# Layer 0 context attention of a four-layer perceiver on Trainium2: features laid out by halves of the heads, rotation without a matmul, the inverse root by logarithm, exponential and a Newton step

## The chip, the cores and the metric

The program runs on one core of one Trainium2 chip. The metric is the device time of one execution in microseconds. The core has a matrix engine (PE, with weight loads PEld beside it), a vector engine (DVE), an activation engine (ACT), a general engine (POOL) and a queue that issues transfers (SP), each working through its own instructions in order; semaphores make one wait for another.

## The reference, cut to what matters

Twelve stages of four layers run one after another on x (4 batches of 256 tokens with 256 features). The change is in the first stage, attention of x to a context of 4 x 4096 rows with 16 heads of 16 features, where queries and keys are normalised and rotated per head:

```python
def rms_norm(x, w):
    var = jnp.mean(x * x, axis=-1, keepdims=True)
    return x * jax.lax.rsqrt(var + EPS) * w

def apply_rope(t, cos, sin):
    t1, t2 = jnp.split(t, 2, axis=-1)
    return jnp.concatenate([t1 * cos - t2 * sin, t2 * cos + t1 * sin], axis=-1)
```

The query (from x) and the key (from the context) of each head go through `rms_norm` and then `apply_rope`; the rest is softmax attention, with scores scaled by a quarter, and an output projection that is added to x.

The other eleven stages are the same in both kernels. Layers 1 and 2 have context attentions of their own, which share code with this one but take its branches without rotation.

## The kernel before, in words

`context_attention` (called by `l0_xattn` with rope=True) works in two steps.

**The projection stage**, `project_first`, makes all queries (2 chunks of 512 columns) and the keys and values of batch 0 (8 chunks). A chunk holds two units, one for each 128 of the 256 features; a unit is 128 features by 512 tokens, and there are 20. For a unit PE multiplies (L1944) and, for keys, makes two tiles of values (L1953); ACT copies the product with the norm's weight (L1979) and squares it (L1980); PE sums the squares within each head by a block matrix (L1933) and exchanges the halves of the heads by a turn matrix (L1934); ACT takes the root of the mean square (L1993); DVE multiplies by cosine (L2009) and, from PSUM, by sine (L2011), adds (L2015) and inverts the root (L2017); POOL applies it (L2041). Then the float32 result is split in three bfloat16 parts, by ACT (L1971), DVE (L2023) and POOL (L2046, L2048), and SP stores them (L1908 for keys, L1913 for queries). The splitting of a unit stands behind the rotation of the next on every engine.

**The batches.** `attend_context` runs once per batch b = 0 to 3. It goes over 16 heads with 8 slots each (e = 0 to 7). In a slot PE makes a 128 x 1024 piece of scores (`scores`, L2343) and weighs the values with the exponentials of the slot before (`weigh`, L2360); ACT takes the exponentials (L2519). Beside that, PE computes the next head's scores a first time (`guard`, 16 pieces of 512 columns per head, L2314, placed by the table GUARDS, up to three per slot), of which DVE takes maxima (L2431). In slot 7 the maxima become a shift (L2328 on PE, the copy L2443 on DVE), and the output of an earlier head is finished (L2373, L2448, L2451). Before the first head a stretch with all 16 guards of head 0 runs alone. SP loads each head's keys, three transfers that each repeat rows of DRAM over several partitions (`load_keys`, L2229): those of head h + 2 once the scores of head h - 1 are done, and in head 15 those of the following batch's first head.

Batches 0 to 2 also make the next batch's keys and values, one unit per head, through the methods of `NextKeys`. Unit h + 1 is made in head h: projection in slots 0 and 1 (L2114), the head sum in slot 2 (`sum_heads`, L2121), the turn in slot 3 (`turn_pairs`, L2126), values in slots 5 and 6 (L2137), all in one PSUM bank. ACT copies and squares (L2151, L2152) before the exponential of slot 2 and takes the root (L2158) before that of slot 3; DVE multiplies by sine (L2182) in slot 4, inverts the root in four quarters (L2188, slots 5 to 7 and 0) and takes the rest (L2194) in slot 3 of the head after; POOL does the cosine product, sum, norm and the two lower parts (L2205 to L2221); SP stores a unit with one transfer (L2099) and loads context and table for two units at a time (L2090, L2095). The order on each engine is written by hand:

```python
if h + 2 < H:
    if h >= 1:
        sp.wait_ge(qk, EU * h)
    load_keys(sp, keys, kstack, h + 2, slot(h + 2), k_in[(h + 2) % 3])
...
if following and h == H - 1:
    new.first_heads_stored(sp)
    sp.wait_ge(qk, EU * (H - 2))
    load_keys(sp, following[1], kstack, 0, slot(H), following_in)
```

`output_product` (L2548 to L2568) ends each batch. Then the next batch's block begins, with the memset L2427 as DVE's first instruction.

## Time and profile before

| what | before |
|---|---|
| median of 3 runs | 7321.39 us (7313.24 to 7321.71) |
| profiled execution, its own time | 7326.7 us |
| span of the profiled execution | 7324.9 us, 101148 instructions |
| busy: PE / DVE / ACT / POOL | 6076.4 / 4217.8 / 3224.1 / 1042.4 us |
| mean granted clock of PE | 0.907 |
| this stage: projection | about 24 to 212 us of the span |
| this stage: batches 0, 1, 2, 3 start at | 212.1, 554.0, 892.8, 1232.2 us |

The profile comes from one execution. An engine is busy while one of its instructions runs; a mean over the span mixes stages with different limits, so a stretch is read by itself. The granted clock is a share of PE's full speed. In a timeline a row gives start, duration, engine, source line, operation, and in brackets the idle time ahead of it and what ended that. Matmuls of float32 count as two records each.

### The profile page before, as it was taken

Reading aid. Unit: us, or ns where it says so; the run is one execution under the profiler, and the core shown is the slowest. Engines: PE = TensorE matmul, PEld = TensorE weight load, DVE = VectorE, ACT = ScalarE, POOL = GpSimd, SP = SyncE. Lnnn points to the kernel's source line nnn. Section 1 sums busy time; section 2 is a strip of 40 time slices with the busy share of each in tenths; the row PEclk is TensorE's granted clock in tenths of the full one; section 3 lists DMA queues with packets and bytes.
Section 4 is the critical chain, followed back from the end, with each engine's and each line's share of the span. In section 5 each row is a group of like instructions: output and inputs, shape, how many; then the busy total and the mean of one; then the engine's idle time right before and its main releaser. Section 6 shows DMA issues by size and latency. Waiting matters only on the chain. (4 is left out here: it accounts for less than half of the span.)

```text
span 7324.9 us, 101148 instructions
## 1 busy us (share of the span) xinstructions
PE 6076.4 (83%) x35500; PEld 3373.9 (46%) x35500; DVE 4217.8 (58%) x8493; ACT 3224.1 (44%) x7821; POOL 1042.4 (14%) x1122
## 2 busy tenths in 40 slices
PE   6799999978288379999998897878877998987887
PEld 3344444423155245454445554333333565556754
DVE  8777787839311236666673332988987445535631
ACT  3566665510033125454453111988987223532211
POOL 4222221004423420000000002110100000001100
PEclk8899999979699689999998898999988678998998
DMA  3323231130288432222210113322321000022100
GB/s 114 92 74 96 78 91 61 51 107 0 99 259 258 134 115 85 75 79 79 64 53 28 36 35 106 97 85 83 97 62 61 1 1 7 1 84 67 49 19 24
DMA packets 281228, 550.02 MB, mean 75 GB/s; under 512 B 29726, under 2 KB 186789, under 8 KB 261909
## 3 DMA queue, kind: packets, MB, share of 16 engines
q1 hardware_dynamic: 262388, 493.46, 22.6%
q0 software_dynamic: 18336, 50.09, 1.9%
q8 instruction: 286, 4.69, 0.3%
q14 instruction: 218, 1.78, 0.1%
HBM read 414.73 MB, written 128.75 MB: 74 GB/s over the span
## 5 line engine op out<-in xcount | busy, mean ns | idle before, releaser
L2431 DVE TENSOR_REDUCE t<-banks 128x1 f32<-128x512 f32 x2048 | 1373.3, 690 | 369.7 <-PE banks L2314 302.8
L2519 ACT ACTIVATE t<-banks 128x1024 f32<-128x1024 f32 x1024 | 1044.2, 1025 | 768.1 <-PE banks L2343 763.3
L2747 ACT ACTIVATE t<-banks,t 128x256 f32<-128x256 f32 x2048 | 939.9, 529 | 77.7 <-DVE t L2684 55.0
L2314 PE MATMUL banks<-t 96*128 96x512 bf16 x2048 | 796.2, 394 | 109.9 <-PEq L66 59.4
L2684 DVE TENSOR_REDUCE t<-banks 128x4 f32<-128x1024 f32 x512 | 623.7, 1219 | 97.3 <-PE banks L2630 56.7
L2360 PE MATMUL banks<-t 128*17 128x256 f32 x8192 | 641.7, 385 | 20.8 <-ACT t L2519 17.5
L2343 PE MATMUL banks<-t 97*128 97x256 bf16 x4096 | 651.4, 273 | 0.0
L2747 ACT ACTIVATION_READ_ACCUMULATOR t<-banks,t 128x1 f32 x2048 | 512.5, 261 | 0.0
L2343 PEld LDWEIGHTS banks<-t 97*128 97x128 bf16 x4096 | 390.6, 98 | 256.7 <-issue 112.2
L2643 PE MATMUL banks<-t 128*17 128x256 f32 x4096 | 327.1, 405 | 160.8 <-DVE t L2695 109.2
L2314 PEld LDWEIGHTS banks<-t 96*128 96x128 bf16 x2048 | 198.7, 97 | 558.6 <-DVE t L2431 333.5
L2630 PE MATMUL banks<-t 96*128 96x256 bf16 x2048 | 328.1, 286 | 50.8 <-PEq L66 25.4
L2219 POOL CAST t<-t 128x512 bf16<-128x512 f32 x144 | 87.7, 609 | 1874.7 <-DVE t L2194 1874.7
L2114 PE MATMUL banks<-xn_feat,t 128*128 128x512 f32 x576 | 321.4, 642 | 13.7 <-issue 6.7
L2137 PE MATMUL banks<-t,xn_feat 128*128 128x256 f32 x1152 | 317.5, 398 | 1.1 <-DVE t L2182 1.1
L1556 ACT ACTIVATE t<-banks,t 128x256 f32<-128x256 f32 (+1 forms) x384 | 171.9, 453 | 331.6 <-DVE t L1522 331.5
L2630 PEld LDWEIGHTS banks<-t 96*128 96x128 bf16 x2048 | 185.1, 103 | 264.5 <-ACT t L2747 155.1
L1522 DVE TENSOR_REDUCE t<-banks 128x1 f32<-128x256 f32 (+1 forms) x384 | 136.6, 398 | 280.8 <-PE banks L1658 158.1
L1198 DVE TENSOR_TENSOR t<-banks,t 128x192 f32<-128x192 f32 x127 | 45.5, 358 | 435.8 <-ACT t L1179 435.8
L2360 PEld LDWEIGHTS banks<-t 128*17 128x17 f32 x8192 | 136.1, 95 | 314.1 <-issue 254.6
L575 PE MATMUL banks<-t 128*128 128x256 f32 x1024 | 239.5, 391 | 32.1 <-DMA t<-in_ctxT 32.1
L2137 PEld LDWEIGHTS banks<-t,xn_feat 128*128 128x128 f32 x1152 | 205.4, 191 | 102.2 <-issue 58.9
(418 smaller groups left out, 10058.8 us busy)
## 6 DMA issues: line engine op xcount, KB each, us to landing
t<-in_L_ffn_w SPq DMA_DIRECT2D x127, 640.0 KB, 5.3
scratch_k<-t SPq DMA_DIRECT2D x192, 384.0 KB, 15.0
t<-scratch_k SPq DMA_DIRECT2D x192, 384.0 KB
t<-scratch_k SPq DMA_DIRECT2D x192, 256.0 KB
xn_feat<-in_ctxT SPq DMA_DIRECT2D x72, 512.0 KB, 15.7
t<-in_ctxT SPq DMA_DIRECT2D x56, 512.0 KB
t<-scratch_k SPq DMA_DIRECT2D x192, 128.0 KB
t<-in_L_ffn_w SPq DMA_DIRECT2D x18, 1024.0 KB
```

The costliest lines, as they stand in the source:

```text
L575: mm = nc.tensor.matmul(out, ctx[:, ch % 2, k, (2 * i + t) * P:(2 * i + t + 1) * P], wkv[:, k, kind * C:(kind + 1) * C], start=k == 0, sto ...
L2114: mm = self.core.nc.tensor.matmul(self.out, self.w[:, k, f * P:(f + 1) * P], self.ctx[:, c % 2, k, :], start=k == 0, stop=k == CT - 1)
L2137: mm = nc.tensor.matmul(self.v_out[:, t * C:(t + 1) * C], self.ctx[:, c % 2, k, (2 * f + t) * P:(2 * f + t + 1) * P], self.w_v[:, k, :], s ...
L2314: mm = nc.tensor.matmul(ps[:, 4 + g % 2, :], qstack[0:SHIFT, h, t * P:(t + 1) * P], kstack[0:SHIFT, slot(h), kc * KC:(kc + 1) * KC], start ...
L2343: mm = nc.tensor.matmul(out, kstack[:, slot(h), kt * P:(kt + 1) * P], qstack[:, h, :], start=True, stop=True, skip_group_check=bool(near))
L2360: mm = nc.tensor.matmul(ps[PART * j:PART * j + VW, OUT, 0:T], v[:, 4 * e + j, h, :], p[:, i % 3, j * T:(j + 1) * T], start=e == 0, stop=e ...
L2431: nc.vector.tensor_reduce(gm[:, h % 2, g // NK, g % NK:g % NK + 1], ps[:, 4 + g % 2, :], AX.X, ALU.max).then_inc(max_done, 1)
L2519: nc.scalar.activation(p[:, i % 3, :].rearrange("p (b t) -> p b t", b=2), ps[:, 2 * (i % 2):2 * (i % 2) + 2, :], ACT.Exp).then_inc(exp_don ...
L2630: mm = nc.tensor.matmul(ps[:, 2 * (i % 3) + j // 2, (j % 2) * T:(j % 2 + 1) * T], kstack[0:SHIFT, slot(h), kt * P:(kt + 1) * P], qstack[0: ...
L2643: mm = nc.tensor.matmul(ps[PART * j:PART * j + VW, OUT, 0:T], scaled[:, i % SL, j, :], p[:, i % SL, j * T:(j + 1) * T], start=e == 0, stop ...
L2684: nc.vector.tensor_reduce(nm[:, i % 4, :], ps[:, 2 * (i % 3):2 * (i % 3) + 2, :].rearrange("p b (j t) -> p (b j) t", j=2), AX.X, ALU.max, ...
L2747: nc.scalar.activation(p[:, i % SL, j * T:(j + 1) * T], ps[:, 2 * (i % 3) + j // 2, (j % 2) * T:(j % 2 + 1) * T], ACT.Exp, bias=nm[:, i % ...
```

## The change

Queries and keys of layer 0 get their features in another order in the weights: the first halves of all 16 heads are unit 0 of a chunk, the second halves unit 1. The partner of a feature in the rotation is then the same partition of the other unit, so the turn matmul goes, and the sine product reads the other unit's copy in SBUF. The head sum becomes one accumulated pair of matmuls per chunk with a block matrix of eights, and root, mean and inverse are made once per chunk. The inverse root is exp(-0.5 ln(m)) on ACT followed by a Newton step of three DVE instructions, in place of a square root and a reciprocal; ln and exp come from one table set, loaded once per phase. In the batches the rotation moves to POOL altogether (six products and sums per chunk, then two for the norm), units run two heads ahead instead of one, and the units of a chunk are stored together, with three transfers per unit instead of one, in every second head. In the projection stage the rotation stays on DVE. The non-rotating branches of `project_first` and `NextKeys` keep their instructions. The core of the diff, stage by stage (projection on PE, ACT and DVE; the new class RopeKeys; then SP, PE, DVE and ACT of `attend_context`; the layout):

```diff
+                    pe.wait_ge(copied, CT * (c + 1))
+                    for f in range(CT):
+                        mm = nc.tensor.matmul(ps[:, 4 + c % 2, :], pairs, square[:, f, :], start=f == 0, stop=f == CT - 1)
...
+                nc.scalar.preload_act_table_set(EXP_AND_LN)
...
+                    act.wait_ge(summed, c + 1)
...
+                    nc.scalar.activation(mean[:, c % 2, :], ps[:, 4 + c % 2, :], ACT.Identity, bias=eps,
+                                         scale=1.0 / D).then_inc(mean_done, 1)
+                    nc.scalar.activation(root[:, c % 2, :], ps[:, 4 + c % 2, :], ACT.Ln, bias=eps,
+                                         scale=1.0 / D).then_inc(log_done, 1)
+                    nc.scalar.activation(root[:, c % 2, :], root[:, c % 2, :], ACT.Exp, scale=-0.5).then_inc(root_done, 1)
...
+                    for f in range(CT):
+                        nc.vector.tensor_tensor(mix[:, s, f, :], raw[:, s, f, :], tab[:, s, 0, :],
+                                                ALU.mult).then_inc(cos_done, 1)
+                    for f in range(CT):
+                        nc.vector.tensor_tensor(spun[:, f, :], raw[:, s, 1 - f, :], tab[:, s, 1, :],
+                                                ALU.mult).then_inc(sin_done, 1)
+                    for f in range(CT):
+                        nc.vector.tensor_tensor(mix[:, s, f, :], mix[:, s, f, :], spun[:, f, :],
+                                                ALU.subtract if f == 0 else ALU.add).then_inc(mixed, 1)
...
+                    link(nc.vector.tensor_tensor(mean[:, s, :], mean[:, s, :], root[:, s, :], ALU.mult))
+                    link(nc.vector.scalar_tensor_tensor(out=mean[:, s, :], in0=mean[:, s, :], scalar=-0.5,
+                                                        in1=root[:, s, :], op0=ALU.mult, op1=ALU.mult))
+                    nc.vector.scalar_tensor_tensor(out=root[:, s, :], in0=mean[:, s, :], scalar=1.5, in1=root[:, s, :],
+                                                   op0=ALU.add, op1=ALU.mult).then_inc(refined, 1)
...
+def half_rows(dest, part, c, f):
+    return dest[part].rearrange("(h two d) n -> two h d n", two=2, d=D // 2)[f, :, :, c * KC:(c + 1) * KC]
...
+    def store(self, sp, u):
+        sp.wait_ge(self.low_done, u + 1)
+        for part in range(3):
+            sp.dma_start(half_rows(self.dest, part, u // CT, u % CT), self.parts[:, u % 2, part, :]).then_inc(
+                self.stored[u % 2], 16)
...
+    def first_heads_stored(self, sp):
+        self.all_stored(sp)
...
+    def product_used(self, pe, u):
+        pe.wait_ge(self.copied, u + 1)
+        if u % CT == CT - 1:
+            pe.wait_ge(self.mean_done, u // CT + 1)
+            pe.wait_ge(self.log_done, u // CT + 1)
...
+            nc.gpsimd.tensor_tensor(self.mix[:, f, :], self.raw[:, f, :], self.tab[:, s, 0, :], ALU.mult).then_inc(
+                self.cos_done, 1)
+            nc.gpsimd.tensor_tensor(self.spun[:, 1 - f, :], self.raw[:, f, :], self.tab[:, s, 1, :], ALU.mult).then_inc(
+                self.sin_done, 1)
...
-                        if (h + 1) % CT == 0 and (h + 1) // CT + 1 < new.chunks:
-                            new.load_chunk(sp, (h + 1) // CT + 1)
-                        new.store(sp, h)
+                        if h % CT == 1 and (h + 3) // CT < new.chunks:
+                            new.load_chunk(sp, (h + 3) // CT)
+                        if h % CT == 0:
+                            for f in range(CT):
+                                new.store(sp, h + f)
...
+                    if new and rope and g in (2, 4):
+                        if g == 4:
+                            new.product_used(pe, 0)
+                        for k in range(CT):
+                            new.multiply(pe, g // 2 - 1, k)
+                    if new and rope and g == 6:
+                        new.sum_heads(pe, 0)
...
-                    u = h + 1
+                    u = h + lead
-                    if new and rope and u < H and e == 2:
-                        new.sum_heads(pe, u)
-                    if new and rope and u < H and e == 3:
-                        new.turn_pairs(pe, u)
+                    if new and rope and u < H and e == 3 and u % CT == CT - 1:
+                        new.sum_heads(pe, u // CT)
...
-                    if new and rope and e == 3:
-                        new.take_rest(dve, u - 1)
-                    if new and rope and u < H and e == 4:
-                        new.scale_sin(dve, u)
+                    if new and rope and h % CT == 0 and e in (4, 6):
+                        new.take_rest(dve, h + (e - 4) // 2)
+                    if new and rope and h % CT == 1 and h + 1 < H and e in (5, 6):
+                        new.refine(dve, e - 5, h // CT + 1)
+                    if new and rope and h % CT == 0 and h >= 2 and e == 0:
+                        new.refine(dve, 2, h // CT)
-                    if new and rope and u < H and e >= 5:
-                        new.invert(dve, u, e - 5)
-                    if new and rope and e == 0:
-                        new.invert(dve, u - 1, 3)
...
+                    w = h + 2
+                    if new and rope and w < H and e == 2:
+                        new.copy_product(act, w)
+                    if new and rope and w < H and w % CT == CT - 1 and e == 4:
+                        new.take_logs(act, w // CT)
...
+    halves = lambda a: cont(a.reshape(C, H, 2, D // 2).transpose(0, 2, 1, 3).reshape(C, C))
+        o["L0_xattn_W" + n] = halves(o["L0_xattn_W" + n])
```

**PE, slots 2 and 3 of a head in the batches.** L2314 and L2515 are guards, L2343 and L2544 scores, L2360 and L2561 weighing. Before, every head:

```order
L2314 MATMUL banks<-t 128x512
L2121 MATMUL banks<-t,block 128x512
L2314 MATMUL banks<-t 128x512
L2343 MATMUL banks<-t 128x256 x4
L2314 MATMUL banks<-t 128x512
L2360 MATMUL banks<-t 17x256 x4
L2314 MATMUL banks<-t 128x512
L2126 MATMUL banks<-t 128x512
L2314 MATMUL banks<-t 128x512
L2343 MATMUL banks<-t 128x256 x4
L2314 MATMUL banks<-t 128x512
L2360 MATMUL banks<-t 17x256 x4
```

Now, in every second head (in the others L2329 is missing):

```order
L2515 MATMUL banks<-t 128x512
L2561 MATMUL banks<-t 17x256 x4
L2515 MATMUL banks<-t 128x512 x2
L2544 MATMUL banks<-t 128x256 x4
L2515 MATMUL banks<-t 128x512
L2561 MATMUL banks<-t 17x256 x4
L2515 MATMUL banks<-t 128x512
L2329 MATMUL banks<-t 128x512 x2
L2515 MATMUL banks<-t 128x512
L2544 MATMUL banks<-t 128x256 x4
L2515 MATMUL banks<-t 128x512
L2561 MATMUL banks<-t 17x256 x4
```

The sum L2121 has moved from slot 2 to slot 3 and stands there twice (L2329, two units); the turn L2126 is gone.

**SP in the batches, between the key loads of successive heads.** L2229 and L2422 load keys, L2099 and L2315 store a unit, L2090, L2095 and L2213, L2310 load context and table. Before:

```order
L2099 DMA scratch_k<-t 128x3x512
L2229 DMA t<-scratch_k 48x1x4096
L2229 DMA t<-scratch_k 32x1x4096
L2229 DMA t<-scratch_k 16x4096
L2090 DMA xn_feat<-in_ctxT 128x2x512
L2095 DMA t<-in_c_rope_k 128x2x512
L2099 DMA scratch_k<-t 128x3x512
L2229 DMA t<-scratch_k 48x1x4096
L2229 DMA t<-scratch_k 32x1x4096
L2229 DMA t<-scratch_k 16x4096
L2099 DMA scratch_k<-t 128x3x512
```

Now:

```order
L2315 DMA scratch_k<-t 16x8x512 x6
L2422 DMA t<-scratch_k 48x1x4096
L2422 DMA t<-scratch_k 32x1x4096
L2422 DMA t<-scratch_k 16x4096
L2213 DMA xn_feat<-in_ctxT 128x2x512
L2310 DMA t<-in_c_rope_k 128x2x512
L2422 DMA t<-scratch_k 48x1x4096
L2422 DMA t<-scratch_k 32x1x4096
L2422 DMA t<-scratch_k 16x4096
L2315 DMA scratch_k<-t 16x8x512 x6
```

The one store after each head's key loads has become six ahead of every second head's, behind the waits for both units of the chunk.

## Rows read from the trace of the kernel before

**Rows 1.** Stretches: us, busy of PE, PEld, DVE, ACT, POOL (instructions), granted clock, DMA share, GB/s
```profile
24.40:194.00 169.60, 115.93 (x295) 60.72 (x293) 145.06 (x101) 56.94 (x100) 72.67 (x60) 0.85 0.36 114
893.00:1232.00 339.00, 315.60 (x2188) 147.70 (x2186) 264.31 (x435) 219.23 (x257) 88.58 (x80) 0.98 0.29 84
```

**Rows 2.** Timeline of DVE and POOL, one unit of the projection stage: start, duration, instruction
```profile
110.12 0.63 DVE L2023 SCALAR_TENSOR_TENSOR t<-t 128x512 f32<-128x512 f32 x1
110.35 1.52 POOL L2041 TENSOR_TENSOR t<-t 128x512 f32<-128x512 f32 x1 [5.60 <-DVE t L2017]
110.95 1.47 DVE L2009 TENSOR_TENSOR t<-t 128x512 f32<-128x512 f32 x1 [0.20 <-DVE t L2023]
111.82 1.07 POOL L2046 CAST t<-t 128x512 bf16<-128x512 f32 x1
112.97 1.15 POOL L2048 TENSOR_TENSOR t<-t 128x512 bf16<-128x512 f32 x1
113.05 1.62 DVE L2015 TENSOR_TENSOR t<-t 128x512 f32<-128x512 f32 x1
114.59 3.34 DVE L2017 RECIPROCAL t<-t 128x512 f32<-128x512 f32 x1
117.86 0.62 DVE L2023 SCALAR_TENSOR_TENSOR t<-t 128x512 f32<-128x512 f32 x1
```

**Rows 3.** The shift copy of each head (L2443), by source line: batch 1, then batch 3
```profile
L2443 DVE CAST t<-banks x16: 429/429/430, 571.5 to 872.6; 1x256 bf16<-1x256 f32 x16
...
L2443 DVE CAST t<-banks x16: 429/430/431, 1245.1 to 1465.0; 1x256 bf16<-1x256 f32 x16
```

**Rows 4.** Timeline of PE, slots 2 to 4 of one head of batch 1
```profile
718.12 0.60 PE L2343 MATMUL banks<-t 97*128 97x256 bf16 x4
720.73 0.60 PE L2343 MATMUL banks<-t 97*128 97x256 bf16 x4
722.75 1.12 PE L2126 MATMUL banks<-t 128*128 128x512 f32 x2 [0.32 <-ACT t L2158]
723.93 0.60 PE L2343 MATMUL banks<-t 97*128 97x256 bf16 x4
725.09 0.63 PE L2360 MATMUL banks<-t 128*17 128x256 f32 x8 [0.34 <-ACT t L2519]
725.87 0.60 PE L2343 MATMUL banks<-t 97*128 97x256 bf16 x4
```

**Rows 5.** Waits of PE in batch 3: us in total, times, longest us
```profile
PE banks L2314 <- DMA t<-scratch_k: 10.0, 12, 3.8
```

**Rows 6.** Timeline at the start of batch 3, SP and PE
```profile
1232.06 3.71 SPq L2229 DMA_DIRECT2D t<-scratch_k  x6
...
1248.87 0.61 PE L2314 MATMUL banks<-t 96*128 96x512 bf16 x1 [3.82 <-DMA t<-scratch_k]
```

**Rows 7.** DMA issues, median us to landing: projection stage, then batch 1
```profile
xn_feat<-in_ctxT SPq DMA_DIRECT2D x1, 512.0 KB, 3.8
...
scratch_k<-t SPq DMA_DIRECT2D x16, 384.0 KB, 4.0
xn_feat<-in_ctxT SPq DMA_DIRECT2D x9, 512.0 KB, 16.2
```

**Rows 8.** Timeline at the end of batch 1 and the start of batch 2
```profile
868.59 1.84 SPq L2229 DMA_DIRECT2D t<-scratch_k  x3
872.57 0.43 DVE L2443 CAST t<-banks 1x256 bf16<-1x256 f32 x1 [1.47 <-PE banks L2328]
885.40 0.38 DVE L2451 TENSOR_SCALAR t<-banks,t 128x16 f32<-128x16 f32 x2
892.79 0.27 DVE L2427 MEMSET banks<- 128x256 f32 x1 [0.79 <-PEq L66]
897.62 3.62 PE L2114 MATMUL banks<-xn_feat,t 128*128 128x512 f32 x4
909.99 0.43 DVE L2443 CAST t<-banks 1x256 bf16<-1x256 f32 x1 [0.69 <-PE banks L2328]
```

More of the change, by code:

```diff
@@ L1848, with project_first @@
 PART = 32
+EXP_AND_LN = "natural_log_exp_and_others"
 def part_columns(dest, c, f):
     return dest[:, f * P:(f + 1) * P, c * KC:(c + 1) * KC].rearrange("s p n -> p s n")
-def project_first(core, wq, queries, q_rope, scale, wk, wv, context, keys, v, k_rope, first, kstack):
+def project_first(core, wq, queries, scale, wk, wv, context, keys, v, first, kstack):
     nc, ps = core.nc, core.ps
-    rope = q_rope is not None
     with ExitStack() as c_:
@@ L2071, in __init__ @@
         self.core, self.w, self.w_v, self.v, self.source, self.dest = core, w, w_v, v, source, dest
-        self.rope, self.out, self.v_out = rope, core.ps[:, spare, :], core.ps[:, v_bank, :]
+        self.out, self.v_out = core.ps[:, spare, :], core.ps[:, v_bank, :]
         self.ctx = core.xnT[:, :, :].rearrange("p a (k n) -> p a k n", k=CT)
         self.rest, self.parts = sb([P, 2, KC]), sb([P, 2, 3, KC], BF16)
-        if rope:
-            self.norm_w, self.table, self.turn, self.eps = rope
-            self.tab = sb([P, 2, 2, KC])
-            self.raw, self.square, self.root, self.mix, self.spun = (sb([P, 2, KC]) for _ in range(5))
@@ L2141, in multiply_values @@
             mm.then_inc(self.v_product, 1)
[L2144 to L2159 removed]
     def whole(self, u):
[L2162 removed]
+        return self.out
     def high(self, engine, u, copy):
[L2165 removed]
+        engine.wait_ge(self.product, u + 1)
         if u >= 2:
@@ L2271, in attend_context @@
             k_in = (k_a, k_b, k_c)
-            new = NextKeys(core, sb, next_sems, spare=SPARE, v_bank=SPARE, **coming) if coming else None
+            new = kind(core, sb, next_sems, spare=SPARE, v_bank=SPARE, **coming) if coming else None
             @block.sync
@@ L2291, in _ @@
                         load_keys(sp, following[1], kstack, 0, slot(H), following_in)
-                    if new:
+                    if new and rope:
+                        if h % CT == 1 and (h + 3) // CT < new.chunks:
+                            new.load_chunk(sp, (h + 3) // CT)
+                        if h % CT == 0:
+                            for f in range(CT):
+                                new.store(sp, h + f)
+                    if new and not rope:
                         if (h + 1) % CT == 0 and (h + 1) // CT + 1 < new.chunks:
@@ L2458, in _ @@
                         new.take_rest(dve, 0)
-                    if new and rope and g == 11:
-                        new.scale_sin(dve, 0)
                 negate(0)
                 place_shift(0)
-                if new and rope:
-                    for quarter in range(3):
-                        new.invert(dve, 0, quarter)
                 for i in range(H * EU):
@@ L2532, in _ @@
                     for u in range(new.units):
-                        if rope:
-                            new.rotate(pool, u)
+                        if rope and u % CT == 0:
+                            new.rotate(pool, u // CT)
+                            new.normalise(pool, u // CT)
                         new.low_parts(pool, u)
@@ L2789, in context_attention @@
                        + ([(eps[:, :], 1e-6)] if rope else []))
-            project_first(core, wq, queries, q_rope, scale, wk, wv, context(0), keys[0], values[0], k_rope,
-                          (queries_of(0), q97[0]), k97)
+            if rope:
+                project_rope(core, wq, queries, q_rope, scale, wk, wv, context(0), keys[0], values[0], k_rope,
+                             (queries_of(0), q97[0]), k97)
+            else:
+                project_first(core, wq, queries, scale, wk, wv, context(0), keys[0], values[0],
+                              (queries_of(0), q97[0]), k97)
         def attend_batch(b, coming):
```

489 lines of the change are left out of this document (308 added, 181 removed).

## The prediction

> **What bounds the kernel now.** I read the busy times by stretch first, then the timelines of the stretches that the change touches. Two kinds of stretch matter; everything after batch 3 of this layer runs the same instructions before and after.
>
> The projection stage lasts some 170 us, and DVE is busy for 145 of them, PE for 116 [rows 1]. Its timeline shows why: from one split (L2023) to the next, 110.12 to 117.86, a unit takes 7.74 us, 3.34 of it the reciprocal [rows 2]. The reader is to see a second thing there. The cosine product L2009, two inputs in SBUF, shows 1.47 us where L2023 shows 0.62. It was issued 0.6 us after POOL's product began, and ends 0.55 us after that one ends (110.35 + 1.52 = 111.87; 110.95 + 1.47 = 112.42). L2015 behaves the same behind POOL's subtraction (112.97 + 1.15 = 114.12, end 114.67). So DVE and POOL take turns here.
>
> Batches 0 to 2 are the other stretch. In batch 2 PE is busy for 316 of 339 us, DVE for 264, ACT for 219, POOL for 89 [rows 1]: PE sets the pace. A head takes (872.6 - 571.5)/15 = 20.07 us with a unit of the next batch's keys in it, and (1465.0 - 1245.1)/15 = 14.66 us in batch 3, which carries none [rows 3]. Within a head, slot 2 (with the head sum) lasts 2.61 us, slot 3 (with the turn L2126) 3.20, slot 4 1.94; in slot 3 PE waits 0.32 us for the square root on ACT, and in slot 4 0.34 us for an exponential that stands behind it and two table loads [rows 4].
>
> Price of a unit's matmul: 20.07 - 14.66 = 5.41 us per head, less those 0.66 us of waiting, is 4.75 us for six pieces of equal column count (two projections, sum, turn, and four value products of half the columns): **0.79 us** each. It is a little low, since batch 3 loses some time to key loads itself [rows 5].
>
> **The change, part by part.**
>
> *Projection stage.* Per pair of units the two reciprocals go, and DVE then runs eleven products of 512 columns whose inputs all lie in SBUF (two cosine, two sine, two sums, three Newton steps, two splits): 11 x 0.63 = 6.9 us. POOL's three instructions per unit run from 110.35 to 114.12, 3.77 us, of which about 0.23 and 0.46 are waits for DVE; 3.1 without them, 6.2 per pair [rows 2]. If the two engines exclude each other, a pair needs 6.9 + 6.2 = 13.1 us; with every POOL duration as recorded, 6.9 + 7.5 = 14.4. If they did not, PE would be next: 115.9/10 = 11.6 us per pair, less two turns, about 9.7. I take the exclusion, because of the ends in [rows 2], and 1 us per pair for hand-overs and for the context load, which stands on SP behind six stores of the older pair instead of two: 14.1 against 15.5. Ten pairs: **-14 us**, with 0 and -58 as the ends.
>
> That choice is also a rule of the Trainium skill, page "SBUF — State Buffer", section "SBUF: two separate sides": DVE and GpSimd share a port pair as an exclusive lock, which a DVE operation with two SBUF inputs needs against a GpSimd operation that reads SBUF. By it the pair costs 13.1 us and more, without it 9.7. The trace agrees, with the two ends above.
>
> *Heads.* Each of the 14 heads with a unit loses its turn and, with the turn, the wait of 0.32; the 0.34 in slot 4 goes with the square root and the table loads. The sum matmuls stay equal in number, but both come in slot 3 of every second head. Per head 0.79 + 0.32 + 0.34 = 1.45 us; 14 heads: **-20.3 us** per batch. If a wait for the logarithms (which PE's value products need) takes the place of the old ones, it is 14 x 0.79 = -11. DVE drops four quarter reciprocals and the sine product per unit and gains three Newton steps per pair; it had 75 us to spare in the batch and gets more, so nothing is gained there. POOL gains two products per pair on 89 us of 339. ACT gains an identity and an exponential per pair and loses four table loads; it is idle for a third of the batch. All of these are covered by PE.
>
> *The unit moved ahead.* The next batch's units now run two heads ahead instead of one, so head 14 carries none: 20.07 - 14.66 = **-5.4 us**. In exchange the stretch before the first shift, 892.79 to 909.99 or 17.2 us [rows 8], takes in a second unit: two projections, a sum, the values (two pieces), less a turn, net four pieces, 3.2 us. There the clock is low: two projection matmuls took 3.62 us [rows 8] instead of 1.6, and DVE's maxima stand behind them. Between 3.2 and about 8; I take **+6 us**.
>
> *End of a batch.* Here a new wait appears. Before, the loads of the following batch's first head were issued at 868.59 in head 14 and the work ended at 885.78, 13.2 us after the last shift copy at 872.57 [rows 8]. Now the halves of a head pair are both needed: SP waits until units 14 and 15 have landed, and unit 15's rest is taken only in slot 6 of head 14. From about the last shift copy: POOL's parts 1 us later, three issues 1.8 us (as three key loads take 1.84 [rows 8]), landing up to 4.0 us [rows 7], then the key loads, whose first head waited from 1232.06 to 1248.87, 16.8 us [rows 6]. Together 21 to 24 us instead of 13.2; since issue and landing overlap I take 20.2: **+7 us**, with +10 as the far end and 0 as the near one.
>
> Per batch -20.3 - 5.4 + 6 + 7 = -12.7, three batches -38; with the projection stage **-52 us**. The profiled execution took 7326.7 us (span 7324.9), so 7274.7; the median of the three runs, 7321.4, lies 5.3 lower, which gives **7269 us**. About 0.2%, 15 us, is what a measurement of this kernel can tell from no change.
>
> **Rivals.**
>
> *Key loads become late, and the kernel slower.* Every second head SP now issues six stores just ahead of a head's key loads, after waiting for the second unit's low part, which ends about 1 us after the last scores of the even head. Key loads land 16.8 us after issue [rows 6]; batch 3, with 14.66 us per head, waits for them 12 times in 16 heads [rows 5], and a context load issued behind them lands after 16.2 us instead of 3.8 [rows 7], so the queue serves in order. A head of 18.6 us and a slot of 1.9 [rows 4], from the last scores to the next use, leave 3.7 us for the delay d. I estimate d at 1.1 + 1.8 and part of a landing, 3 to 4: just covered. With both stores in full ahead, d = 1.1 + 1.8 + 8.0 = 10.9, and PE waits 7.2 us per pair, 14 x 3.6 = 50 us per batch: 7269 + 150 = 7419. From d of about 6 the change loses what it gains. Against it: over two heads, before, the same bytes fitted into 40.1 us with hardly a wait.
>
> The Trainium skill's page "DMA: Bandwidth & Descriptors", section "Why a DMA increments its semaphore by 16 and not by 1", speaks for it: a transfer uses the largest number of engines up to 16 that divides the slowest dimensions of both sides, and the lowest-numbered ones. By it the broadcast key loads run on 3, 2 and 16 engines, so engine 0 carries most of every load. That fits the 16.8 and the 16.2 us; no row here shows single engines.
>
> *Projection stage at PE's pace and no wait at the batch end*: -58, and -20.3 - 5.4 + 6 = -19.7 in each batch: 7321 - 117 = 7204. For it: the tail's waits partly overlap. Against it: [rows 2].
>
> *The gain in heads is half* (-11 per batch), the projection stage gains nothing for want of context, tail +10: -11 - 5.4 + 6 + 10 = -0.4 per batch, so 7320, no change. For it: each new wait stands on an in-order queue.
>
> *The change does not do what it says*: a table load around each logarithm would leave ACT as before. The built order has one load per phase, so this gets next to nothing.
>
> **How the numbers follow.** Forecast (within 30 us of 7269) 0.68; faster rival 0.12; half gain, from there to no change, 0.13; key loads late 0.07, most of it slower. The range from 7228 to 7308 takes in the ends of the terms short of the extremes and leaves out about 2 in 10. Faster by over 0.2%: 0.86; within: 0.09; slower: 0.05.
>
> **What would show it.** In the changed profile: no table load inside the heads; a pair of projection units every 13 to 15 us, with DVE and POOL durations stretched past 0.63 and 1.15; heads alternating around 18.6 us on average, the one with two sums longer; first shift 22 to 25 us after a batch starts; an idle PE of some 7 us before each output product, released by a DMA from scratch_k. Wrong, if PE waits for scratch_k inside the heads, if the pairs come under 11 us apart, or if ACT's new chain shows as PE waits above 0.3 us per head.

## The result and the profile after

The changed kernel takes **7270.95 us** (median of 4 runs, 7268.41 to 7272.54) against 7321.35 before (4 runs): ratio 0.9933, 95% interval 0.9916 to 0.9951, so it is faster by 0.5 to 0.8%. The forecast was 7269 us. The profiled execution took 7272.54 us (span 7270.7) against 7326.7 before, 54 us less. The total fits; its parts do not all fit. Among the runs further down, one of ten of the kernel with few columns in the reciprocals took 8119.73 us at a granted clock of 0.75, and its median is of the other nine.

The two stretches of [rows 1] in the changed kernel, busy time by stretch; columns are us, busy us (instructions) of PE, PEld, DVE, ACT and POOL, granted clock, DMA share, GB/s:

```profile
24.40:195.40 171.00, 93.83 (x254) 51.95 (x252) 92.99 (x110) 65.28 (x111) 73.01 (x60) 0.78 0.40 115
861.80:1186.00 324.20, 302.75 (x2156) 142.29 (x2154) 208.30 (x379) 183.03 (x234) 107.72 (x96) 0.96 0.32 88
```

In the projection stage DVE lost 52 of its 145 us, PE 22 of 116, and the stage is as long as before; no engine is busy for more than 55% of it. In batch 2 DVE lost 56 us, PE 13, and the batch is 15 us shorter.

**Where the time went.** A batch starts with its memset (L2427 before, L2637 after). The start of a batch and its shift copies (L2443 before, L2653 after) cut each batch into three pieces.

| piece, us | before | after | change | forecast |
|---|---|---|---|---|
| batch 0 starts (projection stage and what is ahead of it) | 212.1 | 213.2 | +1.1 | -14 |
| batch start to first shift, batch 1 | 17.5 | 21.9 | +4.4 (+6.4, +6.5 in batches 0, 2) | +6 |
| first to last shift, batch 1 | 301.1 | 272.3 | -28.8 (-30.6, -29.1 in batches 0, 2) | -25.7 |
| last shift to next batch, batch 1 | 20.2 | 29.7 | +9.5 (+6.8, +7.8 in batches 0, 2) | +7 |
| batches 0 to 2 together | 1020.1 | 973.0 | -47.1 | -38 |
| everything after batch 3 starts (same instructions) | 6092.7 | 6084.5 | -8.2 | 0 |

The shift copies of batch 1, by source line, answer to the first of [rows 3]: 272.3/15 = 18.15 us a head against 20.07.

```profile
L2653 DVE CAST t<-banks x16: 429/430/431, 559.6 to 831.9; 1x256 bf16<-1x256 f32 x16
```

**The projection stage waits for its context.** Its waits, all engines (us in total, times, longest):

```profile
POOL t L2172 <- DVE t L2147: 90.7, 10, 17.9
PE banks L2052 <- DMA t<-in_ctxT: 50.9, 4, 15.6
DVE t L2127 <- ACT t L2094: 48.4, 6, 12.2
ACT t L2081 <- DMA scratch_k<-t: 27.5, 8, 10.0
```

The second row has a forerunner in the kernel before, where the same load already held PE up, for less than half the time (24 to 194 us):

```profile
PE banks L1944 <- DMA t<-in_ctxT: 22.5, 6, 4.9
```

SP's own waits in the changed kernel's stretch:

```profile
SPq L2025 <- POOL t L2179: 81.8, 12, 18.0
```

The timeline of one turn of the loop, SP, PE and POOL:

```profile
88.40 4.39 SPq L2025 DMA_DIRECT2D scratch_k<-t  x6
89.47 1.48 POOL L2179 TENSOR_TENSOR t<-t 128x512 bf16<-128x512 f32 x1
...
93.59 1.11 SPq L2013 DMA_DIRECT2D t<-in_ctxT  x1
...
101.25 4.64 PE L2052 MATMUL banks<-t 128*128 128x512 f32 x5 [14.40 <-DMA t<-in_ctxT]
```

The reader is to see an order, not a load: SP waits for POOL's last low part, issues the six stores of the older pair (here, once, a load of queries too), and only then the context load of a pair that PE could long have begun. PE stands still for 14.4 us (15.6, 10.5 and 10.4 us in the three other turns that make up the 50.9), and the eight projection matmuls that follow run mostly at the low level of the clock: 6.03 us for the eight from 101.25, with a granted clock of 0.61, against 3.60 us at 1.00 for the next pair's eight from 112.28. The pairs come 10.5 and 20 to 24 us apart in turn, 15.9 us on average (cosine products L2127 at 74.38, 84.87, 108.57 and, six pairs after the first, 169.63), where 14.1 were forecast and 15.5 stood before.

**The batch end waits for the next keys.** The end of batch 1 answers to [rows 8]:

```profile
830.00 5.27 SPq L2315 DMA_DIRECT2D scratch_k<-t  x6
831.91 0.43 DVE L2653 CAST t<-banks 1x256 bf16<-1x256 f32 x1 [0.72 <-PE banks L2529]
837.14 1.90 SPq L2422 DMA_DIRECT2D t<-scratch_k  x3
844.41 0.38 DVE L2661 TENSOR_SCALAR t<-banks,t 128x16 f32<-128x16 f32 x2
854.76 1.09 PE L2763 MATMUL banks<-ident,t 128*128 128x128 f32 x4 [10.60 <-PEq L66]
```

The key loads for batch 2 are issued 5.2 us after the last shift instead of 4.0 us before it (868.59 against 872.57 [rows 8]). The head's own work ends at 844.8, and PE then idles 10.6 us at the phase's end (9.9 and 10.1 in batches 0 and 2), until 17.6 us after the key loads were issued (16.8 in [rows 6]).

### The profile page after: what moved, and what is told of

It reads as the page before. It is cut to its first block and busy times, and to the rows that moved or that the text cites. A ratio compares the mean times of both kernels' runs of the same rounds, so it can differ in the third digit from the quotient of the medians.

```text
span 7270.7 us, 100659 instructions
## 1 busy us (share of the span) xinstructions
PE 6009.5 (83%) x35364; PEld 3348.9 (46%) x35364; DVE 3997.9 (55%) x8335; ACT 3123.7 (43%) x7764; POOL 1100.0 (15%) x1170
## 5 line engine op out<-in xcount | busy, mean ns | idle before, releaser
L2515 PE MATMUL banks<-t 96*128 96x512 bf16 x2048 | 790.6, 394 | 116.4 <-PEq L66 68.1
L2544 PE MATMUL banks<-t 97*128 97x256 bf16 x4096 | 650.7, 273 | 0.0
L2561 PE MATMUL banks<-t 128*17 128x256 f32 x8192 | 641.9, 385 | 4.9 <-ACT t L2701 2.9
L2544 PEld LDWEIGHTS banks<-t 97*128 97x128 bf16 x4096 | 390.3, 98 | 231.8 <-issue 92.4
L2515 PEld LDWEIGHTS banks<-t 96*128 96x128 bf16 x2048 | 198.8, 97 | 581.3 <-DVE t L2641 360.0
L1198 DVE TENSOR_TENSOR t<-banks,t 128x192 f32<-128x192 f32 x127 | 45.4, 358 | 436.0 <-ACT t L1179 436.0
L2561 PEld LDWEIGHTS banks<-t 128*17 128x17 f32 x8192 | 136.5, 95 | 288.2 <-issue 255.2
## 6 DMA issues: line engine op xcount, KB each, us to landing
scratch_k<-t SPq DMA_DIRECT2D x128, 384.0 KB, 15.6
xn_feat<-in_ctxT SPq DMA_DIRECT2D x72, 512.0 KB, 15.9
```

The lines of the kernel that those rows point to most:

```text
L2515: mm = nc.tensor.matmul(ps[:, 4 + g % 2, :], qstack[0:SHIFT, h, t * P:(t + 1) * P], kstack[0:SHIFT, slot(h), kc * KC:(kc + 1) * KC], start ...
L2544: mm = nc.tensor.matmul(out, kstack[:, slot(h), kt * P:(kt + 1) * P], qstack[:, h, :], start=True, stop=True, skip_group_check=bool(near))
L2561: mm = nc.tensor.matmul(ps[PART * j:PART * j + VW, OUT, 0:T], v[:, 4 * e + j, h, :], p[:, i % 3, j * T:(j + 1) * T], start=e == 0, stop=e ...
```

## The experiments

Eleven kernels ran: five edit the changed kernel, six the kernel before. Where an edit adds lines, the line numbers of its profile move by a few.

### Context ahead of the stores

```diff
-                for c in range(C_ALL + 2):
+                for c in range(C_ALL + 3):
...
-                    if c >= 2:
+                    if c >= 3:
                         for f in range(CT):
-                            u = CT * (c - 2) + f
+                            u = CT * (c - 3) + f
```

> The changed kernel, but in layer 0's projection SyncE issues the context and table loads of chunk c ahead of the stores of chunk c-3, instead of behind those of chunk c-2 (the stores lag one chunk more). Nothing else moves. Theory (the projection gained nothing because each context load is queued behind six stores that wait for GpSimd): the idle time of TensorE ended by the context's landing (50.9 us, 4 times, in the changed kernel) falls below 20 us, the pairs come every 13 to 15 us instead of 10.5 and 20 to 24 in turn, batch 0 starts 12 to 20 us sooner than 213.2 us, and the time is about 7254 us (7250 to 7260). Rival 1 (the exclusion of VectorE and GpSimd bounds the pairs as they are, the context's landing only takes the blame): batch 0 starts at most 5 us sooner, 7266 to 7272 us. Rival 2 (the stores that come later hold up the high parts on ScalarE, which wait for the buffer): no gain or a loss, with ScalarE idle behind the DMA into scratch_k for over 30 us.

Measured: **7233.26 us** (7228.20 to 7237.33), ratio to before 0.9878 (0.9862 to 0.9895); batch 0 starts at 180.2, 33 us sooner than in the changed kernel; the batches are as they were (18.13 us a head). The waits of the stage:

```profile
POOL t L2172 <- DVE t L2147: 53.2, 10, 15.9
ACT t L2081 <- DMA scratch_k<-t: 33.9, 14, 7.8
...
PE banks L2052 <- DMA t<-in_ctxT: 1.9, 1, 1.9
```

The wait for the context fell from 50.9 to 1.9 us, and the pairs now come 12.0 us apart (L2127 at 75.52 and, five pairs on, at 135.72). The theory stands, and its size was too small by half. It had 13 to 15 us a pair from DVE and POOL by turns; 12.0 lies below the 13.1 of that sum without any hand-over, so the two run beside each other for part of the time. The granted clock of the stage rose from 0.78 to 0.86 with PE's idle time gone.

### The next batch's keys in two pieces

```diff
+                    if following and rope and h == H - 2:
+                        for f in range(CT):
+                            sp.wait_ge(new.stored[f], 16 * 3 * (new.units // 2 - 1))
+                        sp.wait_ge(qk, EU * (H - 2))
+                        load_key_columns(sp, following[1], kstack, slot(H), following_in, 0, S - KC)
+                    if following and rope and h == H - 1:
+                        new.first_heads_stored(sp)
+                        load_key_columns(sp, following[1], kstack, slot(H), following_in, S - KC, S)
```

> The changed kernel, but the key load of the following batch's first head is split by columns: the columns of the first 14 units are loaded while head 14 runs, and only the last 512 columns wait for the last two units' stores. Theory (the 8.5 us that each batch's end grew is the key load waiting for the last unit's stores and its landing of about 16 us): the stretch from the last shift copy of a batch to the next batch's memset falls from 28.7 to between 19 and 23 us in batches 0 to 2, 18 to 28 us in all, and the time is about 7247 us (7242 to 7254). Rival (the end grew because head 14's and the output product's own work moved there, and the key load only lands in its shade): 28 us as before, time 7268 to 7274 us.

Measured: **7240.32 us** (7234.81 to 7244.62), ratio 0.9889 (0.9873 to 0.9906); last shift to next memset 19.9, 20.0 and 19.8 us. PE's wait at the phase's end in batch 1 is 1.6 us in place of 10.6:

```profile
PE banks L2778 <- PEq L66: 1.6, 1, 1.6
```

So the whole growth of the batch's end was the key load; the rival falls. The gain, 30.6 us, is somewhat more than the 28 us of the tails and than the theory's range (7242 us at the least).

### Both

The diff is the two above together.

> Both of the edits before this one together. Theory: the places are 200 us apart and share nothing, so the gains add: about 7230 us (7222 to 7242). Rival (either gain is given back in the other's place, or neither exists): within 5 us of the better of the two alone.

Measured: **7213.06 us** (7207.36 to 7215.22), ratio 0.9853 (0.9837 to 0.9869): 58 us below the changed kernel, where the two alone gave 38 and 31, so the gains add but for some 10 us. The forecast of 7222 to 7242 was missed on the low side, because each gain was larger than its own forecast. In the profiles batch 3 starts at 1125.6 against 1186.2, 60.6 us sooner; 34.2 and 32.4 with each edit alone. Most of the 6 us missing there is seen: from memset to first shift the three batches together take 69.3 us in the changed kernel, 67.8 and 66.2 with one edit alone, and 69.4 here. That piece has two lengths in all these runs, and they go with the clock. In the changed kernel, PE's timeline at the start of batch 0 and of batch 1:

```profile
216.82 3.78 PE L2232 MATMUL banks<-xn_feat,t 128*128 128x512 f32 x4 [1.12 <-DMA xn_feat<-in_ctxT]
221.87 3.74 PE L2232 MATMUL banks<-xn_feat,t 128*128 128x512 f32 x4 [0.41 <-ACT t L2346]
...
541.36 3.78 PE L2232 MATMUL banks<-xn_feat,t 128*128 128x512 f32 x4 [1.38 <-DMA xn_feat<-in_ctxT]
546.40 1.98 PE L2232 MATMUL banks<-xn_feat,t 128*128 128x512 f32 x4 [0.41 <-ACT t L2346]
```

The first four run at a granted clock of 0.50 in both batches. The second four run at 0.52 in batch 0 and at 1.00 in batch 1, the low and the high level of the clock (1.2 and 2.4 GHz), 1.8 us apart, and these pieces take 23.7 and 21.9 us. Why the clock rises sooner in one than in the other was not tried.

### One table

```diff
-        self.core.nc.scalar.activation(self.root[:, u % 2, :], self.out, ACT.Sqrt, bias=self.eps,
+        self.core.nc.scalar.activation(self.root[:, u % 2, :], self.out, ACT.Exp, bias=self.eps,
```

> The kernel before, but the root of the batches' key units is taken with ScalarE's exponential in place of its square root (so the inverse root is wrong in value): same instruction count and shape, but ScalarE need not load a table on its way there and back. Everything else, the turn matmul, the eight reciprocals, the order, stays. Theory (in the heads about a third of the gain was TensorE's wait behind ScalarE's root, the price of the table loads): 0.5 to 0.7 us a head, 24 to 32 us of the 45 heads with a unit, time 7290 to 7300 us. Rival (TensorE's waits in those slots end with something else that is as late, and the heads' gain is the turn matmul alone): at most 0.1 us a head, 7317 to 7324 us.

Measured: **7275.10 us** (7272.91 to 7279.94), ratio 0.9937 (0.9921 to 0.9954). Heads take 19.08, 19.17 and 19.15 us against 20.18, 20.07 and 20.07. No wait of PE for ACT is left in batch 1; 0.66 us a head had been listed, and 0.9 to 1.1 went, more than the 0.5 to 0.7 of the theory. PE's timeline of the slots of [rows 4] shows why:

```profile
602.80 0.60 PE L2343 MATMUL banks<-t 97*128 97x256 bf16 x4
604.33 1.02 PE L2126 MATMUL banks<-t 128*128 128x512 f32 x2
605.41 0.60 PE L2343 MATMUL banks<-t 97*128 97x256 bf16 x4
606.94 0.60 PE L2343 MATMUL banks<-t 97*128 97x256 bf16 x4
```

Slot 3 is 605.41 - 602.80 = 2.61 us against 3.20, slot 4 is 1.53 against 1.94: 0.59 and 0.41 us shorter where the profile lists waits of 0.32 and 0.34. The matmuls beside a wait lose their overlap as well, and the listed idle time leaves that out: the turn starts 0.23 us after the start of the guard ahead of it, which takes 0.39 (604.10 to 604.33), where before it started 0.71 us after (722.04 to 722.75), and it takes 1.02 us against 1.12 in [rows 4]. This one edit, without the changed kernel's other parts, gains 0.63% where the whole change gains 0.67%, though the change gives some of it back at the batches' ends.

### A narrow turn

```diff
-        self.core.nc.tensor.matmul(self.out, self.turn, self.raw[:, u % 2, :], start=True, stop=True).then_inc(
+        self.core.nc.tensor.matmul(self.out[:, 0:16], self.turn, self.raw[:, u % 2, 0:16], start=True, stop=True).then_inc(
```

> The kernel before, but the turn matmul of the batches' key units covers 16 of its 512 columns (31 of 32 columns of the turned raw values are left out). It still waits for the root and is waited for. Theory (the turn is on TensorE's path at its full price of 0.79 us): 0.7 to 0.8 us a head, 31 to 36 us over 45 heads, time 7284 to 7292 us. Rival (TensorE has slack there, since it waits for the root anyway): under 0.3 us a head, 7308 to 7322 us.

Measured: **7342.42 us** (7334.94 to 7346.53), ratio 1.0030 (1.0019 to 1.0041): less work, and slower. Neither theory had that. PE's waits between the first and last shift of batch 1 (577 to 890.7):

```profile
PE banks L2360 <- ACT t L2519: 15.9, 15, 1.1
PE banks L2126 <- ACT t L2158: 4.8, 15, 0.3
```

Before, the first row was 5.0 us in 15 heads. The turn's own groups, of the kernel before and of this one (columns: busy us, mean ns, idle time ahead of them):

```profile
L2126 PE MATMUL banks<-t 128*128 128x512 f32 x30 | 16.9, 645 | 4.8 <-ACT t L2158 4.8
```

```profile
L2126 PE MATMUL banks<-t 128*128 128x16 f32 x30 | 5.9, 273 | 4.8 <-ACT t L2158 4.8
```

The turn gave up 16.9 - 5.9 = 11.0 us, and the wait for the exponential behind the table loads grew by 10.9: the turn's time came back as ACT's lateness to the last tenth. The loss of 12.6 us in the 15 heads goes with the clock. The four largest of PE's other groups (guards, scores, weighted sums, values) grew from 91.9, 72.1, 74.5 and 33.9 us to 95.2, 75.7, 77.8 and 36.2, 12.5 together, with the same instructions; and in three of seven stretches of 21 us, about a head each, the granted clock is 0.84, 0.92 and 0.92, where the kernel before had 1.00 over the same heads:

```profile
577.00:598.00 21.00, 17.43 (x100) 7.80 (x104) 15.98 (x24) 11.88 (x14) 5.53 (x5) 0.84 0.16 61
...
640.00:661.00 21.00, 19.38 (x143) 9.63 (x143) 17.21 (x29) 13.80 (x18) 5.54 (x5) 1.00 0.43 107
...
682.00:703.00 21.00, 19.38 (x132) 8.85 (x133) 16.37 (x27) 13.07 (x16) 5.53 (x5) 0.92 0.43 107
```

In one of the heads that lost it, PE waited 1.06 us for the exponential (until 633.64), and the granted clock was 0.50 from 634.0 to 637.0. The same wait in the next head (until 655.21) left it at 1.00, so a wait does not bring the fall each time, and what decides it stays open.

### Few columns in the reciprocals

```diff
-        part = self.root[:, u % 2, quarter * P:(quarter + 1) * P]
+        part = self.root[:, u % 2, quarter * P:quarter * P + 8]
```

> The kernel before, but each of the four reciprocal quarters of the batches' key units covers 8 of its 128 columns (15 of 16 of the inversion is left out); 3.34 us of VectorE's time a unit goes to about 0.4. Theory (the heads are bound by TensorE, VectorE's relief is worth nothing by itself): within 0.1 us a head, time 7315 to 7325 us. Rival (VectorE's relief is what paid in the changed kernel): 1 us a head or more, 7276 us or less.

Measured: **7306.11 us** (median of nine, 7295.79 to 7310.27), ratio 0.9981 (0.9971 to 0.9991). Heads of 19.83 to 19.99 us, 0.1 to 0.3 less; PE's waits for ACT are as before (5.0 and 4.8 us in 15 heads). VectorE's relief alone is worth a fifth of a per cent: a little more than the theory, far less than the rival.

### Tables and turn together

The diff is the two edits (one table, narrow turn) together.

> The edits of e4_one_table and e5_narrow_turn together, on the kernel before. Theory (the turn was hidden in TensorE's wait for ScalarE, so that alone it gave nothing, and the narrower turn even lost the clock; with ScalarE in time it is on the path): heads of 18.2 to 18.6 us against 19.1 with the tables alone and 20.07 before, 24 to 40 us below e4_one_table's 7275, time 7235 to 7251 us. Rival (the narrow turn costs clock by itself, or TensorE has slack in that slot): heads of 19.0 us or more, time 7272 to 7300 us.

Measured: **7266.49 us** (7264.89 to 7270.74), ratio 0.9928 (0.9913 to 0.9943); heads of 19.05, 18.84 and 18.84 us. Both missed: with the tables gone the turn gives 0.3 us a head in two batches and nothing in the first, not 0.5 to 0.9. PE's waits between the first and last shift of batch 1 show a new one:

```profile
PE banks L2314 <- DVE t L2431: 4.1, 16, 0.3
```

With ACT in time, the score banks that PE fills next are still being read by DVE's maxima. The granted clock over the heads is 0.99 to 1.00 here with the same narrow turn, so it is not the narrow matmul by itself that cost the clock above.

### All three, and the sine product

The first adds the few columns in the reciprocals (and takes ACT's identity in place of the exponential); the second narrows DVE's sine product as well:

```diff
-        self.core.nc.vector.tensor_tensor(self.spun[:, u % 2, :], self.out, self.tab[:, u // CT % 2, 1, :],
+        few = KC if u < 2 else 8
+        self.core.nc.vector.tensor_tensor(self.spun[:, u % 2, 0:few], self.out[:, 0:few], self.tab[:, u // CT % 2, 1, 0:few],
```

> The kernel before with the three relieved at once in the batches' key units: no table load (ScalarE's identity in place of the square root, so the root is left out), 16 of 512 columns of the turn, 8 of 128 columns of each reciprocal quarter. Theory (TensorE, ScalarE and VectorE stood within a few tenths of a microsecond of each other in a head, so that a third relief pays what two could not: the waits for VectorE's maxima, 0.25 to 0.3 us a head in e9_table_and_turn, go): heads of 18.3 to 18.6 us against 18.84 there; the changed kernel's 15 intervals with one unit fewer, 18.14 + 5.4/15, stand for 18.5; time 7245 to 7260 us. Rival (the rest of the changed kernel's gain in the heads comes from the pairing of the units, not from VectorE): heads of 18.8 us or more, 7262 to 7270 us.

> The kernel of e10_all_three, and VectorE's sine product of the batches' key units covers 8 of 512 columns from the third unit of a batch on (63 of 64 columns left out). In e10_all_three the wait of 0.25 us stayed: VectorE worked without a pause from the rest's subtraction through the sine product, two products of 0.68 us among four maxima of a slot and the next. Theory (the sine product in that place, which the changed kernel moves to another slot, is the last 0.25 us): the waits behind the maxima fall from 16 to at most 3 in 15 heads, heads of 18.3 to 18.6 us, time 7240 to 7250 us. Rival (TensorE's own work fills the head: the wait goes and the time stays): heads of 18.7 us or more, 7252 to 7262 us.

Measured: **7255.48 us** (7254.41 to 7270.13), ratio 0.9920 (0.9903 to 0.9937), heads of 18.65, 18.74 and 18.75 us; and **7263.75 us** (7248.48 to 7267.76), ratio 0.9925 (0.9908 to 0.9941), heads of 18.55, 18.67 and 18.59 us. The two times cannot be told apart, and the wait stayed in both. The first time lies in its theory's range, but its heads and its wait do not bear the theory out; the second lies above both of its ranges. The second run's row, batch 1:

```profile
PE banks L2315 <- DVE t L2432: 4.0, 16, 0.3
```

So neither the reciprocals nor the sine product is its cause, and that theory falls. DVE's timeline in the first of the two shows another product in front of the wait, the subtraction of the high part (L2194), in the slot that the narrow turn shortened:

```profile
615.16 0.69 DVE L2431 TENSOR_REDUCE t<-banks 128x1 f32<-128x512 f32 x1 [0.19 <-PE banks L2314]
615.77 0.68 DVE L2194 TENSOR_TENSOR t<-t 128x512 f32<-128x512 f32 x1
616.37 1.28 DVE L2431 TENSOR_REDUCE t<-banks 128x1 f32<-128x512 f32 x2
```

That product and the two maxima behind it are 1.9 us of DVE (615.77 to 617.65), as long as PE's whole slot now lasts (613.43 to 615.32). That reading was not tried. A second candidate for what still parts these heads from the changed kernel's is the narrowed turn itself, which holds PE for another 0.14 us a head (from its start at 614.96 to the next guard's at 615.10).

### Few columns on GpSimd

```diff
-                        nc.gpsimd.tensor_tensor(mix[:, c % 2, f, :], mix[:, c % 2, f, :], root[:, c % 2, :],
+                        nc.gpsimd.tensor_tensor(mix[:, c % 2, f, 0:8], mix[:, c % 2, f, 0:8], root[:, c % 2, 0:8],
```

and the same for the middle and the low part.

> The kernel of e1_ctx_ahead, but GpSimd's three products of a projection unit cover 8 of 512 columns (from the second pair on), so 63 of 64 columns of the normalising, the middle and the low part are left out in that stage. Same instructions, same waits. Theory (VectorE's two-input products are stretched because GpSimd runs beside them): the pairs of cosine and sine products, 2.3 to 2.7 us in e1_ctx_ahead where GpSimd runs, take 1.29 us throughout, and the splits 0.69 each. Rival (they are stretched by the tables' and the context's landing in the same buffers, or by TensorE and ScalarE): 2.3 us and more in half of the pairs or more. The time also shows what GpSimd's share of the loop is worth: 5 us or less if ScalarE's wait for the stores sets the pair, 20 us or more if GpSimd and VectorE by turns set it.

Measured: 7211.72 us (2 runs); batch 0 starts at 152.3 us, 28 sooner than at 180.2; pairs 8.9 us apart (L2127 at 79.65 and, four on, at 115.14). The cosine and sine products of one pair, first with GpSimd's full columns (context ahead), then with few:

```profile
112.09 2.49 DVE L2127 TENSOR_TENSOR t<-t 128x512 f32<-128x512 f32 x2 [1.29 <-ACT t L2094]
114.51 2.66 DVE L2132 TENSOR_TENSOR t<-t 128x512 f32<-128x512 f32 x2
```

```profile
89.53 1.29 DVE L2127 TENSOR_TENSOR t<-t 128x512 f32<-128x512 f32 x2 [1.48 <-ACT t L2094]
90.74 1.29 DVE L2132 TENSOR_TENSOR t<-t 128x512 f32<-128x512 f32 x2
```

Every pair but one takes 1.28 to 1.31 us. The one, at 46.58 and 49.03, takes 2.52 and 2.66, and beside it GpSimd makes the parts of the first pair with all their columns (46.39 to 51.14). So the stretching is GpSimd's work beside it, as the prediction took from the ends in [rows 2]. The Trainium skill's page "SBUF — State Buffer", section "SBUF: two separate sides", states that exclusion of a VectorE operation with two SBUF inputs and a GpSimd one that reads SBUF; these rows agree, 2.5 against 1.29. With few columns on GpSimd the stage goes at about PE's pace, the end of -58 us that the prediction kept for the case without exclusion (212 - 58 = 154). The 28 us are not the exclusion's alone: GpSimd's own time in the chain of a pair went as well.

### Three buffers for the parts

```diff
-        rest, parts, ctx = sb([P, 2, KC]), sb([P, 2, 3, KC], BF16), sb([P, 2, CT, KC])
+        rest, parts, ctx = sb([P, 2, KC]), sb([P, 3, 3, KC], BF16), sb([P, 2, CT, KC])
...
-                    if u >= 2:
-                        act.wait_ge(stored[u % 2], 16 * stores_of(u))
+                    if u >= 3:
+                        act.wait_ge(stored[u % 3], 16 * stores_of(u))
```

> The kernel of e3_both with three buffers in place of two for the parts of a projection unit, so that the high part of unit u waits for the stores of unit u-3 instead of u-2 (room for it: the mean is kept once instead of twice). Theory (with the context in time, the pair's loop is ScalarE's high part waiting for the stores of the pair before, 45 us in e1_ctx_ahead): ScalarE's waits for the DMAs into scratch_k and scratch_q fall below 30 us, batch 0 starts 6 to 15 us sooner than 179.5 us, time 7196 to 7207 us. Rival (VectorE and GpSimd, by turns, are as late): waits move to VectorE behind GpSimd, batch 0 starts at most 3 us sooner, time 7209 to 7216 us.

Measured: **7205.40 us** (7193.83 to 7209.32), ratio 0.9836 (0.9823 to 0.9850). Batch 0 starts at 177.5 us, only 2 sooner; ACT's waits for the stores fell from 45.4 to 36.7 us (27.7 and 9.0), not below 30. The time lies in the theory's range, but by place the rival is right: DVE and POOL are nearly as late, as the run with few GpSimd columns also shows. The median lies 8 us below that of both edits, but the two intervals overlap, and the stage accounts for 2 us of it.

**The version to keep** is the changed kernel with the context ahead and the keys split, 7213 us, 1.3 to 1.6% below the kernel before and 58 us below the change; a third buffer may add a little.

## Why the prediction was right, and where it was not

**The time, 7269 against 7270.95, is right by luck: parts cancel.** Two parts were 9 and 15 us off in opposite directions, and 8 us came from stretches with the same instructions; the runs of one kernel differ by as much.

**Projection stage, -14 forecast, +1 measured: the step that failed.** The exclusion of DVE and POOL was read rightly for DVE's products of two inputs in SBUF, and the run with few GpSimd columns shows it; as a sum of both engines' times it was too high, since the pairs came 12.0 us apart with the context ahead, where that sum gave 13.1. What failed is the charge for the rest, "1 us per pair for hand-overs and for the context load, which stands on SP behind six stores of the older pair instead of two". That sentence named the mechanism that then set the stage, and priced it as a hand-over. The runs showed a whole extra link of the loop in its place: POOL's last low part, six issues of 4.39 us, a context load that PE can use 7.7 us after its issue (93.59 to 101.25; 4.5 us in the turn at 127.08), and PE's work at the low clock. The third rival had it ("gains nothing for want of context"), tied to a halved gain in the heads that did not come. With the order mended the stage gains 33 us, so what was lost is more than the whole forecast term. One of the prediction's signs of being wrong, pairs under 11 us apart, came in every second pair (10.5), yet it does not speak against the exclusion: the other pairs came 20 to 24 us apart, waiting for their context.

**Heads, -25.7 forecast, -28.8 to -30.6 measured: right mechanism, two sizes off.** The waits of 0.66 us were worth 0.9 to 1.1 with the overlap around them. The turn's 0.79 could not be added to them as a sum: alone it was worth nothing, and with the tables gone at most 0.3, because PE, ACT and DVE stood within a few tenths of a microsecond of each other in these slots. The prediction had it that in the heads "DVE drops four quarter reciprocals and the sine product per unit" and that "nothing is gained there". Alone the reciprocals give 0.1 to 0.3 us a head. With ACT relieved and the turn narrowed PE waits for DVE's maxima, and the changed kernel, which has DVE's products in other slots, shows 0.5 us of that wait in 15 heads. At 18.15 us a head, and 18.15 + 5.4/15 = 18.5 with a unit in each, it is still a little below all the partial edits; whether DVE's order or the rest of the narrowed turn makes the last 0.05 to 0.2 us stays open.

**First shift later, +6 forecast, +4.4 to +6.5 measured.** Right, the low clock with it.

**Batch end, +7 forecast, +6.8 to +9.5 measured.** Right in mechanism and size; the split load takes all of it back. PE idles 10.6 us there instead of about 7, and the profile puts the wait down to the phase's end (PEq), not to a DMA from scratch_k as the prediction had it, since SP holds the phase open for the load.

**Key loads in the heads.** PE has no wait for scratch_k between the first and last shift of batches 0 to 2, so the slower rival and its order of stores ahead of key loads did not come: the delay stayed below the 3.7 us that the prediction found to spare. In that rival "engine 0 carries most of every load" does not follow from the prediction's own 3, 2 and 16 engines, which would give engine 0 a third, a half and a sixteenth of the three loads; no run here shows single engines. What the changed kernel does with ACT is what the change says: 31 table loads, 39.7 us, stood in the heads of batch 1 before, none after.

```profile
L2519 ACT ACT_TABLE_LOAD x16 | 20.5, 1283 | 0.3
L2158 ACT ACT_TABLE_LOAD x15 | 19.2, 1283 | 0.3
```

## What to carry to other kernels

When a change makes a queue's group of waiting commands larger, draw the loop that goes through that queue before pricing its instructions: here six stores ahead of one load cost 33 us, all that the engines had saved, and moving the load ahead gave it back. A load for the next stage that waits for the last piece of its data can be split, so that only that piece is late. Where three engines stand within tenths of a microsecond of each other, single savings neither add up nor show alone: relieving ACT was worth 44 us, DVE's reciprocals 13, and narrowing PE's turn lost 24, with the clock.

## What the runs showed that was not expected

Taking work from TensorE can make it slower: a narrower matmul in each of 15 heads (30 records) left its time as waiting (0.34 to 1.06 us a head), the granted clock over the heads fell from 1.00 to 0.96, and a head took 0.5 to 0.9 us longer. A listed wait can understate its cost: 0.32 and 0.34 us of idle time beside matmuls were worth 0.59 and 0.41 when they went. And a table load on ScalarE took 1.28 us, with 0.3 us of idle time ahead of 15 or 16 of them together; ScalarE is idle for a third of a batch, and yet its table loads cost 44 us, through the exponential queued behind them.
